# Graph layer kernel: GpSimd's bias add for the node tiles moves to the beginning of its step

## The reference

```python
h = jnp.maximum(_layernorm(x, axis=-1), 0.0)
rel_inputs = concatenate([h[src], h[dst], edge_attr], axis=-1)      # per edge
rel_effects = relu(rel_inputs @ re_w1 + re_b1) @ re_w2 + re_b2
agg_effects = segment_sum(rel_effects, dst, num_segments=50000)     # per node
effect_inputs = concatenate([h, agg_effects], axis=-1)
updated = relu(effect_inputs @ ea_w1 + ea_b1) @ ea_w2 + ea_b2
return x + updated
```

## Time and profile before

| | |
|---|---|
| time, median of 3 runs | 955.74 us (954.33 to 956.46) |
| the profiled execution's own time | 956.01 us |
| its span, first to last instruction | 954.1 us |
| mean granted clock of TensorE | 0.987 of full speed |
| PE, DVE, POOL, ACT busy | 97%, 78%, 64%, 63% of the span |

### The profile page before, as it was taken

One profiled execution on the slowest core, in us unless ns is written; L12 is line 12 of the kernel. 1 busy time (PEld: TensorE's weight loads), 2 busy tenths in 40 slices (PEclk: granted clock), 3 DMA queues, 4 the chain that ended last, 5 costly groups with the idle time before them and its releaser, 6 DMA issues.

```text
span 954.1 us, 21049 instructions
## 1 busy us (share of the span) xinstructions
PE 923.3 (97%) x6450; PEld 817.8 (86%) x6450; DVE 740.1 (78%) x2155; ACT 605.5 (63%) x1180; POOL 609.1 (64%) x600
## 2 busy tenths in 40 slices
PE   4879999999999999999999999999999999999987
PEld 4668998898898899889889889988988988998876
DVE  5887788788788878878877887886887788788562
ACT  1447666666666766666666676666666667666653
POOL 7785776776677677677667767767766776772320
PEclk7979999999999999999999999999999999999999
DMA  6253655555565565555556556555555655554442
GB/s 200 75 148 113 183 163 168 150 177 175 151 186 168 151 183 163 168 151 176 172 155 185 167 153 183 162 169 158 169 174 151 186 167 152 169 177 146 124 123 76
DMA packets 114105, 151.88 MB, mean 159 GB/s; under 512 B 17984, under 2 KB 70080, under 8 KB 113984
## 3 DMA queue, kind: packets, MB, share of 16 engines
q1 hardware_dynamic: 101440, 124.73, 43.2%
q0 software_dynamic: 12544, 25.72, 10.2%
HBM read 104.92 MB, written 45.46 MB: 158 GB/s over the span
## 4 chain that ended last, share of the span: by engine, by line
PE 94%; DVE 3%; SPq 1%; issue 1%; ACT 1%; DMA 0%; DVEq 0%
PE l_ps L531 33%; PE l_ps L546 27%; PE l_ps L536 17%; PE agg_ps L496 7%; PE edge_ps L479 4%; PE node_ps L487 4%; PE node_ps L471 1%; SPq L294 0%; DVE rel_row L831 0%; DVE hot L844 0%; SPq L300 0%; DVE lo L804 0%; DVE h L797 0%; DMA drow_i<-in_dst_rows 0%; DMA win<-rel_rows 0%
## 5 line engine op out<-in xcount | busy, mean ns | idle before, releaser
L386 POOL DMA_INDIRECT gath<-in_x,dst_all x196 | 200.2, 1022 | 59.7 <-issue 59.7
L386 POOL DMA_INDIRECT gath<-in_x,src_all x196 | 195.0, 995 | 52.9 <-issue 51.7
L546 PE MATMUL l_ps<-w2n,hid 128*128 128x128 f32 x1568 | 193.6, 277 | 0.0
L655 ACT ACTIVATE hid<-l_ps,b1n 128x512 f32<-128x512 f32 x196 | 135.0, 689 | 82.4 <-PE l_ps L536 82.4
L409 POOL TENSOR_TENSOR ea_lo<-ea_in,ea_hi 128x512 fp32r<-128x512 f32 x45 | 74.3, 1651 | 171.6 <-ACT ea_hi L629 171.6
L546 PEld LDWEIGHTS l_ps<-w2n,hid 128*128 128x128 f32 x1568 | 182.9, 192 | 0.1
L810 DVE SCALAR_TENSOR_TENSOR lo<-node_ps,hi 128x512 fp32r<-128x512 f32 x98 | 67.3, 687 | 146.1 <-ACT hi L638 146.1
L663 ACT ACTIVATE h<-xin,shift,rs 128x128 f32<-128x128 f32 x392 | 165.2, 486 | 0.0
L531 PE MATMUL l_ps<-hi,w1n_hi 128*128 128x512 f32 x392 | 155.7, 397 | 0.4 <-ACT hid L655 0.4
L531 PE MATMUL l_ps<-hi,w1n_lo 128*128 128x512 f32 x392 | 155.4, 396 | 0.0
L402 POOL TENSOR_TENSOR xb<-xin,b2n 128x512 f32<-128x512 f32 x98 | 131.0, 1354 | 33.5 <-DVE res L838 33.5
(11 more groups left out here) (98 smaller groups left out, 1566.1 us busy)
## 6 DMA issues: line engine op xcount, KB each, us to landing
win<-rel_rows SPq DMA_DIRECT2D x392, 98.0 KB
xin<-in_x_tiles SPq DMA_DIRECT2D x98, 256.0 KB, 4.2
out<-res SPq DMA_DIRECT2D x98, 256.0 KB, 3.4
rel_rows<-rel_row SPq DMA_DIRECT2D x49, 392.0 KB, 2.4
ea_in<-in_ea_t SPq DMA_DIRECT2D x49, 256.0 KB, 3.2
gath<-in_x,src_all POOLq DMA_INDIRECT x196, 2.7
gath<-in_x,dst_all POOLq DMA_INDIRECT x196, 2.9
w1e<-in_L_gnn_re_w SPq DMA_DIRECT2D x1, 384.0 KB, 3.6
```

Of the source, the lines that this page charges most:

```text
L386: nc.gpsimd.indirect_dma_start(gath[b][:, s, k, :], None, x, bass.IndirectOffsetOnAxis(ap=idx[:, e * T + k:e * T + k + 1], axis=0)).then_i ...
L546: last = nc.tensor.matmul(l2_ps[turn % 2][:, k * P:(k + 1) * P], hid[r][:, c, k * P:(k + 1) * P], w[:, c, :], start=(c == 0), stop=(c == C ...
L655: nc.scalar.activation(hid[r][:, c, :], l1_ps[c][:, :], ACT.Relu, bias=b[:, c:c + 1]).then_inc(hid_set, 1)
```

## The change

In POOL's joint step the two `keep_x` go from the end of the step to its beginning, ahead of `set_dst`, the gathers and `low_ea`. The condition `j + 1 < NJ` is dropped; it holds in all joint steps.

```diff
             def joint_step(e, j):
+                for r in (1, 2):
+                    keep_x(r, j + 1, True)
                 set_dst(e)
                 if e + 2 < EG:
                     gather(e + 2)
                 if e + 1 < EG:
                     low_ea(e + 1)
-                if j + 1 < NJ:
-                    for r in (1, 2):
-                        keep_x(r, j + 1, True)
```

## The result

The changed kernel takes 1048.19 us (median of 6 runs, 1046.31 to 1051.98), the kernel before beside it 955.9 us (6 runs). The ratio is 1.0971, with a 95% interval of 1.0949 to 1.0993: 92 us slower, where 958.2 was forecast with a range up to 963.5. The profiled execution took 1051.98 us and its span is 1050.2 us.

The account below looks back on a forecast made before the run. PE at full clock was taken to set the 18.35 us period; steady steps and last steps 0, entry +2.44: 956.01 + 2.44 = 958.45 profiled, less 0.27 gives a 958.2 us median, range 955.2 to 963.5.

Parts of the forecast that it names:

- The wait at the entry: Before the first joint step: L831 waits through four `xb`, ending at 64.03 instead of 61.59, 2.44 us later.
- the sum: Whole kernel: 954.10 span + 1.91 = 956.01, + 2.44 = 958.45; median 0.27 below the profiled run: 958.2 us.
- POOL's timetable: Steady joint step: second `xb` at 495.61, copy 496.85, first gather 497.19, eighth 505.98, 12.6 us later than before.
- the late normalising: Steady steps, DVE's L797: moves by about 1.05 us because of the second `xb`, at no cost.
- the landings: Steady steps: last gather landed at 508.9, latest 509.5, wanted by DVE's statistics at 510.4; cover 0.9 to 1.5 us.
- SP's queue: Steady steps: edge-row store waits for L831 anyway, x loads for an `xb` made a step earlier; no cost.
- The ring: Steady-step loop of gathers, statistics, L838, `xb`, gathers: 16.8 to 17.4 us, under PE's period, so lateness dies out.
- rival 2: Steady steps: L797 holds off POOL's copy and first gather, POOL becomes the bound; 983 to 1010 us, chance 0.05.
- Steady steps: 0 us: All joint steps after the entry: moving POOL's work leaves PE's 18.35 us period unchanged, cost 0 us.
- rival 3: Steady steps, small covers break: L831 0.6 late, PE loses 0.1 to 0.2 every second step; 960 to 968, chance 0.14.
- the main case: Steady steps: stretched eighth gather, `ea_lo` starts inside L831 and is held about half a microsecond, cover left 0.9.
- every-second-step: Steady steps: POOL is 0.6 later in the next step and doesn't collide, so loss comes 23 times, 2 to 5 us.

Follow-up runs that it names:

- entry_only: Kernel before, with the new order (both `xb` ahead of copy and gathers) in the first joint step alone; 958.51 us, ratio 1.0029.
- one_early: Kernel before, with only the first tile's `xb` moved to the beginning of the joint step, the second left at its end; 956.84 us, ratio 1.0015.
- gate_both: Changed kernel, with `ea_lo` made to wait until DVE's second remainder (L831) of the same step is done; 959.59 us, ratio 1.0043.
- repaired: Changed kernel, with the old order in the first joint step and `ea_lo` waiting for DVE's second remainder from the second on; 955.81 us, ratio 0.9999.
- stt: Changed kernel, with DVE's second remainder (L830) written as scalar_tensor_tensor in place of tensor_tensor; 1047.34 us, ratio 1.0959.
- gap_xb: Changed kernel, with POOL's first `xb` of a step waiting for POOL's own `ea_lo` to be done; 993.14 us, ratio 1.0386.
- gap_entry: Kernel before, with the second of the two `xb` at the end of the last edge step waiting for the first; 955.20 us, ratio 0.9997.

## Why the prediction was wrong

**Right.** The wait at the entry: L830 to 64.06 (64.03 forecast), PE's dense work 2.5 us later (2.44). Its cost was a little more, 2.9 (1.8 to 3.8) in entry_only, as the next step was 0.45 longer at the lower clock, for which the sum had no term; one_early, with three `xb`, has 1.2. POOL's timetable: second `xb` 4.88 into step 4 (4.90 worked out), first gather 6.45 (6.48), eighth 15.24 (15.27). Nothing of L788, the late normalising, the landings or SP's queue costs time (gate_both, repaired). The ring is shorter than the period (gate_both, 18.35), and rival 2's starved copy didn't come: copy and gathers keep their times beside L796.

**Wrong: "Steady steps: 0 us"**, by three steps in the argument. The term at fault is the hold of DVE's L831, put at nothing in the main sum and at 0.6 us in rival 3; the runs show 1.84 us at first and 2.53 us in the usual step.

1. *Who waits.* "`ea_lo` then starts inside L831 (507.45 to 508.14) and is held about half a microsecond". In 28 steps of the kernel after `ea_lo` came 0.13 to 0.15 behind the start of L830, and each time L830 was the one held. So the main case had the wrong engine waiting. In step 4 it did not even come: it needed a gather to be stretched. The eighth starts at 15.24 of the step, 0.11 ahead of L826, and nothing had stretched POOL. Rival 3, with 0.14, had the case that came there: it has `ea_lo` at 16.23 (measured 16.21) and L831 held. Its "the eighth gather ends before L827" was misread from its own rows (505.98 + 0.94 is 0.17 behind L827's end); measured, it is 0.14 behind.
2. *The size of the hold.* Rival 3 has L831 "held to 508.8, 0.6 late", through `ea_lo` alone. Measured, it was held through the `xb` behind too, and was 1.84 late in step 4 and 2.53 in the usual later step. I had taken the boundary between `ea_lo` and an `xb` as open, from one `hot` of the kernel before. That reading was right for the kernel before, where `hot` gets in there 14 times of 14; what I had overlooked is what stands ahead of `ea_lo`, an idle POOL there and a gather here.
3. *"In the next step POOL is 0.6 later and doesn't collide."* Lateness of L830 isn't left behind by POOL. L837, the second `xb`, the gathers and `ea_lo` stand behind it, and so all of them come later by as much, the next L830 with them. The two orders keep in step: L830 starts 0.13 before `ea_lo` at 18.7 into the step, and is held for 3.2 us, each time. The loss is 2.53 less 0.53 of slack = 2.0 a step. The period's mean is 20.43, as in some steps `hot` is held (2.44) in place of L830 and the step takes 23.14, mostly with a stretch at half clock in it, the next 18.34. 44 times 2.08 is 91.5 us, where rival 3 had 2 to 5.

The slack that rival 3 was built on (0.54) was right within 0.01. With the hold at its true size, 1.84, the first step would have read 1.3 us lost, as it was (19.66 instead of 18.35), and every-second-step at that size, 30 us, would have been outside the range.

**Where POOL's run begins.** In the kernel before, `hot` did get in between `ea_lo` and `xb`; in the kernel after, L830 didn't, and stt shows that it isn't the kind of instruction. The 14 traces part the two cases without an exception, if one asks what stood ahead of POOL's run of `ea_lo` and `xb`. I count the boundaries inside such runs at which a DVE instruction was waiting:

| ahead of the run | between POOL's two instructions | DVE got in |
|---|---|---|
| a gather | no pause | 0 of 94 |
| a gather | a pause of 0.08 us (gap_xb, gap_entry) | 42 of 42 |
| idle time | no pause | 142 of 142 |

An example of the third line of the table is step e = 26 of the kernel before, with its rows: the two `xb` behind `ea_lo` start 0.04 before its recorded end, and `hot` still gets in and stretches the first of them to 1.74.

```profile
499.15 2.97 POOL L402 TENSOR_TENSOR xb<-xin,b2n 128x512 f32<-128x512 f32 x2
```

This is read from the traces and not tried: no run puts idle time ahead of `ea_lo` in the new order without moving something else, and the DVE instructions differ (L831 and L830 in the first two lines of the table, `hot`, shift and normalising in the third). Why a gather ahead should matter is open.

## What to carry to other kernels

Where two engines shut each other out, the price of a collision can be the whole gapless run of the other engine's instructions, not the one that overlaps; look at what stands right behind it, and at what stands ahead: here the run was closed behind a gather and open behind idle time. An idle gap on an engine off the critical path can be what keeps two such engines apart: before filling it, list what of the other engine falls under the work as it will lie. And ask of a collision whether what is late moves the colliding work too; if it does, the cost is paid in each step, and a single wait that fixes the order may take it away.

## What the runs showed of the hardware

A DVE instruction with two SBUF inputs waited through two, three and four `xb` of POOL back to back (2.35, 3.55 and 4.77 us instead of 0.69), always to 0.5 to 0.6 us after the last. All these runs of POOL begin right behind a gather. With POOL pausing about 0.1 us between two instructions it got in (gap_xb, gap_entry).

By the records, the first one to start isn't always the one that goes on (the profile's times for POOL are rough, so 0.1 us is little). Behind a gather, L830 started 0.13 to 0.15 before `ea_lo` and waited, 28 times of 28. Against a POOL that comes from idle it went on: in 12 steps of the kernel after it starts 0.05 before an `xb`, takes 0.69, and the `xb` 1.77 to 1.79, as in step 25 above. So it is for `hot` in the kernel before. The view of `ea_lo`'s line there, and one step:

```profile
L409 POOL TENSOR_TENSOR ea_lo<-ea_in,ea_hi x45: 1283/1848/1867, 76.0 to 883.2; 128x512 fp32r<-128x512 f32 x45
```

```profile
571.30 1.85 POOL L409 TENSOR_TENSOR ea_lo<-ea_in,ea_hi 128x512 fp32r<-128x512 f32 x1 [3.55 <-ACT ea_hi L629]
...
571.32 0.68 DVE L844 SCALAR_TENSOR_TENSOR hot<-node_no,win 128x512 bf16<-128x512 f32 x1
```

`hot` starts 0.02 after `ea_lo` and takes its normal 0.68; `ea_lo` is stretched to 1.85, as in 29 of the 43 steps in which they meet. In all 29 `hot` starts at most 0.03 after `ea_lo`; in the other 14 it starts later and waits. From the kernel before this looked like an even exchange of small delays, and nothing warned of 3.2 us.

The Trainium skill, page "SBUF — State Buffer", section "Who interferes with whom", says that the second of the two waits until the first finishes, and that the order of issue decides, not the shape of the operation. That the shape doesn't decide, stt agrees with (3.22 us in another form). With the rest the traces agree where POOL comes from idle: the engine that starts first, to within 0.03 us, goes on, and DVE waits for one instruction. Right behind a gather they differ: DVE waited for up to four instructions, and an earlier start of 0.13 us didn't win.
